# Graph attention and experts on one Trainium2 core: TensorE works in even steps of two second-layer tiles, two picked columns and one first-layer slice, with one signal per step

## The reference

```python
# x: 6250 x 256; 100000 edges src -> dst
x = x + gnn(layernorm(x))              # graph attention, 4 heads of 64
xn = layernorm(x)                      # what both parts below start from
# a second graph attention makes the expert scores, 4 heads x 4 experts
h = (xn @ W_gat).reshape(M, 4, 4)
e = leaky_relu(a_src[src] + a_dst[dst]); alpha = softmax of e over the edges with one dst
agg = segment_sum(h[src] * alpha, dst) + b_gat
scores = layernorm(agg, ln_gamma, ln_beta).reshape(M, 4, 4).mean(1)
w, i = softmax(top_2(scores))
for ei in range(4):                    # the experts, 256 -> 512 -> 256
    g = w where i == ei
    out += g * (gelu(xn @ W1[ei] + b1[ei]) @ W2[ei] + b2[ei])
return x + out
```

## Time and profile before

| what | value |
|---|---|
| median of 3 runs | 4049.74 us (4045.44 to 4051.8) |
| the profiled execution | 4058.66 us, its span 4057.0 us |
| busy in the span | PE 1940.2 us (48%), DVE 1968.4 (49%), POOL 1737.6 (43%), ACT 663.5 (16%) |
| stretch of the 7 rounds | 2071 us to 3776 us |
| last units after the rounds | 3776 us to 3896 us |

### The profile page before, as it was taken

The page is one execution under the profiler, slowest core; times in us unless marked ns, Lnnn a source line. Parts: engine busy times, 40 slices in busy tenths (PEclk is TensorE's granted clock), DMA queues, the critical chain, the costliest instruction groups (busy, mean ns, idle before and its releaser), DMA issues.

```text
span 4057.0 us, 25978 instructions
## 1 busy us (share of the span) xinstructions
PE 1940.2 (48%) x7318; PEld 1438.6 (35%) x7322; DVE 1968.4 (49%) x3777; ACT 663.5 (16%) x1401; POOL 1737.6 (43%) x1787
## 2 busy tenths in 40 slices
PE   4415044444334353546541395554657565556425
PEld 3311033233223132324430374443546454444314
DVE  7876776645656653446520163233334343233646
ACT  7300021122112121212310011010101011011003
POOL 0015765655565444540777314344442424343241
PEclk9758566666666676767565697777878787777757
DMA  3211344544455343434621011111110111111415
GB/s 123 36 48 28 87 157 152 164 155 154 137 170 164 113 145 121 160 116 168 178 77 8 13 37 27 26 22 22 31 31 29 28 31 25 24 22 25 180 55 211
DMA packets 154183, 354.73 MB, mean 87 GB/s; under 512 B 55510, under 2 KB 96518, under 8 KB 144406
## 3 DMA queue, kind: packets, MB, share of 16 engines
q1 hardware_dynamic: 68303, 196.54, 13.5%
q0 software_dynamic: 69936, 121.07, 12.7%
q10 hardware_dynamic: 15866, 36.29, 2.3%
HBM read 181.01 MB, written 172.19 MB: 87 GB/s over the span
## 4 chain that ended last, share of the span: by engine, by line
PE 18%; another core or an unknown queue 16%; issue 10%; DVE 7%; ACT 1%; DMA 1%; POOL 0%; ACTq 0%; SPq 0%; DVEq 0%; POOLq 0%
PE ffn_psY L1512 7%; PE ffn_psH L1498 6%; PE pick_rows L858 3%; DVE pick_prod L888 1%; DVE at_ring L897 1%; DVE at_ring L692 1%; PE mid_psH L1424 1%; PE mid_psT L1181 1%; DVE pick_hot L874 0%; POOL acc L979 0%; DVE xnT L1715 0%; DVE at_high L662 0%; PE pick_node L839 0%; DVE at_ring L684 0%
## 5 line engine op out<-in xcount | busy, mean ns | idle before, releaser
L618 POOL DMA_INDIRECT at_ring<-table,e_col x768 | 725.9, 945 | 1061.2 <-DMA at_sums<-at_ring 831.2
L2057 POOL DMA_INDIRECT at_ring<-table,at_idx x693 | 671.9, 970 | 585.1 <-DMA at_sums<-at_ring 378.4
L2149 PE MATMUL at_psS<-at_ring,at_hot 128*128 128x260 f32 x1584 | 495.1, 475 | 437.4 <-issue 268.9
L1498 PE MATMUL ffn_psH<-xnT,ffn_space 128*128 x896 | 405.3, 605 | 452.5 <-ACT ffn_space L1539 289.4
L888 DVE SCALAR_TENSOR_TENSOR pick_prod<-const_iota,pick_tile,pick_rows 128x400 f32<-128x400 f16 x256 | 158.5, 629 | 831.1 <-remote 547.5
L2149 PEld LDWEIGHTS at_psS<-at_ring,at_hot 128*128 128x128 f32 x1584 | 346.9, 236 | 575.3 <-issue 351.3
L1512 PE MATMUL ffn_psY<-ffn_space 128*128 128x256 f32 x1568 | 387.7, 405 | 286.4 <-DVE ffn_space L1570 271.9
L1498 PEld LDWEIGHTS ffn_psH<-xnT,ffn_space 128*128 128x128 f32 x896 | 271.9, 312 | 553.8 <-ACT ffn_space L1539 301.0
L1512 PEld LDWEIGHTS ffn_psY<-ffn_space 128*128 128x128 f32 x1568 | 314.9, 204 | 345.8 <-DVE ffn_space L1570 285.8
L2171 ACT ACTIVATE at_ring<-at_psS 128x520 f32<-128x520 f32 (+1 forms) x432 | 238.7, 567 | 768.0 <-PE at_psS L2149 354.6
L1539 ACT ACTIVATE ffn_space<-ffn_psH,ffn_b 128x448 f32<-128x448 f32 x224 | 141.5, 634 | 1056.4 <-DMA at_sums<-at_ring 790.7
(11 more groups left out here) (404 smaller groups left out, 2432.6 us busy)
## 6 DMA issues: line engine op xcount, KB each, us to landing
at_sums<-at_ring SPq DMA_DIRECT2D x72, 1452.0 KB
products<-ffn_space ACTq DMA_DIRECT2D x28, 512.0 KB
at_ring<-table,e_col POOLq DMA_INDIRECT x867
at_sums<-at_ring SPq DMA_DIRECT2D x16, 768.0 KB, 3.2
late_space<-products SPq DMA_DIRECT2D x24, 512.0 KB, 7.9
at_ring<-table,at_idx POOLq DMA_INDIRECT x693
products<-ffn_space ACTq DMA_DIRECT2D x28, 384.0 KB
late_space<-products SPq DMA_DIRECT2D x24, 384.0 KB, 9.8
```

Source lines behind the costliest of these rows:

```text
L618: g.indirect_dma_start(self.ring[z][:, k, 0:TW], None, self.table, bass.IndirectOffsetOnAxis(ap=self.runs.col[:, u * U + k:u * U + k + 1], ...
L1498: last = pe.matmul(self.psH[part][:, 0:half], self.w1[:, k, e * HID + f:(e + 1) * HID:FT], self.xnT[:, k, bass.ds(r * (BT * P) + part * ha ...
L2057: g.indirect_dma_start(self.ring[z][:, k, 0:self.TW], None, self.table, bass.IndirectOffsetOnAxis(ap=self.idx[:, z, k:k + 1], axis=0)).the ...
L2149: last = pe.matmul(self.psS[at % 2][:, k - lo, 0:TW], self.hot[:, b, k, :], rows[:, b * self.SUB + k, 0:TW], start=True, stop=True)
```

## The change

PE's work of a round becomes 16 equal steps (`STEPS`). In step s it makes one pair of second-layer tiles of five steps earlier (`product`, `PAIRS`: 2, 2, 2 and 1 tiles, both tiles of a pair in one bank), then two picked columns, then slice s of the first layer (`hidden`), and raises one semaphore, `s_step`, once. ACT waits for it and does both gelus of the step; DVE waits for it and does the step's two picks (`take`), one addition over the pair (`add`), and the rest of the pick (`put`). `s_h`, `s_y`, `s_out` are gone, and `s_node` is raised only once, at the start. PE still waits for `s_hid`, `s_kept`, `s_hot` and `s_prod`, which ACT and DVE raise. The steps run on over the rounds' border (the second layer of a round's last expert is made in the next round); round 0 stands outside of the loop.

`weigh` is cut in two parts, and `scores` and `weigh` stand after other steps: for unit 2r - 1 after steps 3, 5 and 6 of round r, for unit 2r after steps 10, 11 and 13. Before, unit 2r was weighed at the start of round r + 1. After the rounds, six more steps finish the products, and the last 20 picked columns go four to a signal, over `pick_rows` and the two `psH` banks. SP's early loads for the mixing start after 14 stored units, not 12.

```diff
     def weigh(self, v, u):
+        self.weigh_first(v, u)
+        self.weigh_second(v, u)
+
+    def weigh_first(self, v, u):
...
-        last.then_inc(self.s_node, 1)
+        return last
...
-        for k in range(2 * half, 2 * half + 2):
-            self.column(pe, k, i % 2, k, r * self.ROUND + (i * self.COLS + k + 1))
-
-    def column(self, pe, n, z, k, kept):
+        for k in range(2):
+            pe.wait_ge(self.s_kept, r * self.ROUND + (slot * 2 + k + 1))
+            last = self.column(pe, self.ps_rows[k], i % 2, half * 2 + k)
+        return last
...
-        last.then_inc(self.s_out, 1)
-
-    def late_tensor(self, pe, rounds):
...
+        for k in range(self.COLS):
+            n = chunk * self.COLS + k
+            if not first or k < self.BANKS:
+                pe.wait_ge(self.s_kept, self.BANKS + n - (self.BANKS if first else self.COLS) + 1)
+            last = self.column(pe, banks[k], chunk % 2, k)
+        return last
...
+    def take(self, v, slot, banks):
+
+        S, D = self.SPAN, self.D
+        tiles = self.c["iota16"][:, 0:S].unsqueeze(1).to_broadcast([P, D, S])
+        for k in range(2):
+            n = slot * 2 + k
+            v.scalar_tensor_tensor(out=self.prod[:, k, :, :], in0=tiles, scalar=self.tile[:, n:n + 1],
+                                   in1=banks[k][:, 0:S * D].rearrange("p (d s) -> p d s", d=D),
+                                   op0=ALU.is_equal, op1=ALU.mult).then_inc(self.s_kept, 1)
+
+    def put(self, v, att, slot):
...
-    BT = 7
+    BT, LAG = 7, 5
     HALVES = ((0, 4), (4, 7))
+    PAIRS = ((0, 2), (2, 4), (4, 6), (6, 7))
...
+    def hidden(self, pe, r, s):
+
+        FT, K, BT, HID, half = self.FT, self.K, self.BT, self.HID, self.BT * P // 2
+        e, f = divmod(s, FT)
+        for part in range(2):
+            pe.wait_ge(self.s_hid, r * (2 * self.STEPS) + (2 * s + part + 1))
+            for k in range(K):
+                last = pe.matmul(self.psH[part][:, 0:half], self.w1[:, k, e * HID + f:(e + 1) * HID:FT],
+                                 self.xnT[:, k, bass.ds(r * (BT * P) + part * half, half)],
+                                 start=(k == 0), stop=(k == K - 1))
+        return last
+
+    def product(self, pe, r, n):
+
+        FT, DIM = self.FT, self.DIM
+        e, j = divmod(n % self.STEPS, FT)
+        lo, hi = self.PAIRS[j]
+        pe.wait_ge(self.s_prod, r * self.STEPS + (n + 1))
+        for t in range(lo, hi):
+            for f in range(FT):
+                last = pe.matmul(self.psY[j % 2][:, (t - lo) * DIM:(t - lo + 1) * DIM],
+                                 self.hid[:, e % 2, f, t * P:(t + 1) * P], self.w2[:, e * FT + f, :],
+                                 start=(f == 0), stop=(f == FT - 1))
+        return last
+
+    def tensor(self, pe, picks):
+
+        pe.wait_ge(self.s_w, 16 * (self.K + 1))
+        for s in range(self.STEPS):
+            if s == self.LAG:
+                pe.wait_ge(self.s_w2, 16)
+            if s >= self.LAG:
+                self.product(pe, 0, s - self.LAG)
+            self.hidden(pe, 0, s)
+            picks(0, s).then_inc(self.s_step, 1)
+        with pe.Fori(1, self.rounds) as r:
+            for s in range(self.STEPS):
+                self.product(pe, r, s - self.LAG)
+                picks(r, s)
+                self.hidden(pe, r, s).then_inc(self.s_step, 1)
+
+    def end_tensor(self, pe, s):
+
+        if s == self.LAG - 4:
+            self.freed_by_scalar(pe)
+        self.product(pe, self.rounds, s - self.LAG)
...
+        for s in range(self.STEPS):
+            self.activate(a, 0, s)
+            beside(0, s)
+            if s > self.LAG:
+                self.store(a, 0, s - self.LAG - 1)
+        with a.Fori(1, self.rounds) as r:
+            for s in range(self.STEPS):
+                self.activate(a, r, s)
+                beside(r, s)
+                self.store(a, r, s - self.LAG - 1)
...
+    def activate(self, a, r, s):
+        half = self.BT * P // 2
+        e, f = divmod(s, self.FT)
+        a.wait_ge(self.s_step, r * self.STEPS + (s + 1))
+        for part in range(2):
+            a.activation(self.hid[:, e % 2, f, part * half:(part + 1) * half], self.psH[part][:, 0:half],
+                         ACT.Gelu, bias=self.b1[:, s:s + 1]).then_inc(self.s_hid, 1)
+
+    def store(self, a, r, n):
+
+        e, j = divmod(n % self.STEPS, self.FT)
+        if j % 2:
+            (lo, hi), s_kept = self.HALVES[j // 2], self.s_kept[j // 2]
+            a.wait_ge(self.s_prod, r * self.STEPS + (n + 3))
+            a.dma_start(self.products[bass.ds(r + n // self.STEPS, 1), :, e, lo:hi, :].rearrange("o p t d -> (o p) t d"),
+                        self.prod[:, lo:hi, :]).then_inc(s_kept, 16)
...
+    def add(self, v, n):
+
+        e, j = n // self.FT, n % self.FT
+        lo, hi = self.PAIRS[j]
+        if j % 2 == 0:
+            v.wait_ge(self.s_kept[j // 2], 16 * e + 16)
+        v.tensor_tensor(self.prod[:, lo:hi, :], self.psY[j % 2][:, 0:(hi - lo) * self.DIM].rearrange("p (t d) -> p t d", d=self.DIM),
+                        self.b2[:, e % self.E, :].unsqueeze(1).to_broadcast([P, hi - lo, self.DIM]), ALU.add)\
+            .then_inc(self.s_prod, 1)
...
-                        att.sync(sp, lambda: mix.begin(sp, ffn), ffn.rounds * 2 - 2)
+                        att.sync(sp, lambda: mix.begin(sp, ffn), ffn.rounds * 2)
...
+                        def step(i):
+                            v.wait_ge(ffn.s_step, i + 1)
+                            pick.take(v, i, pick.ps_rows)
+                            if 0 <= i - ffn.LAG < ffn.steps:
+                                ffn.add(v, i - ffn.LAG)
+                            pick.put(v, att, i)
+
+                        def late_chunk(c):
+                            v.wait_ge(ffn.s_step, slots + c - slots // 2 + 1)
                             for half in range(2):
-                                ffn.vector(v, r, e, half)
-                                picked()
+                                pick.take(v, 2 * c + half, late_banks[2 * half:2 * half + 2])
+                                pick.put(v, att, 2 * c + half)
 
                         for r in range(ffn.rounds):
-                            hidden((lambda: att.weigh(v, 2 * r - 2)) if r else None)
-                            hidden(None, (lambda: att.scores(v, 2 * r - 1)) if r else None)
-                            products(r, 0)
-                            hidden(None, (lambda: att.weigh(v, 2 * r - 1)) if r else None)
-                            products(r, 1)
-                            if r == 0:
-                                spread.vector(v)
-                            hidden(None, lambda: att.scores(v, 2 * r))
-                            products(r, 2)
-                            products(r, 3)
+                            for s in range(ffn.STEPS):
+                                step(r * ffn.STEPS + s)
+                                if r and s == 3:
+                                    att.scores(v, 2 * r - 1)
+                                if r and s == 5:
+                                    att.weigh_first(v, 2 * r - 1)
+                                if r and s == 6:
+                                    att.weigh_second(v, 2 * r - 1)
+                                if r == 0 and s == 9:
+                                    spread.vector(v)
+                                if s == 10:
+                                    att.scores(v, 2 * r)
+                                if s == 11:
+                                    att.weigh_first(v, 2 * r)
+                                if s == 13:
+                                    att.weigh_second(v, 2 * r)
...
+                        for i in range(ffn.steps, slots):
+                            step(i)
+                            if i == ffn.steps:
+                                att.scores(v, last - 2)
+                            if i == ffn.steps + 2:
+                                att.weigh_first(v, last - 2)
+                            if i == ffn.steps + 3:
+                                att.weigh_second(v, last - 2)
+                        chunks = range(slots // 2, pick.chunks)
+                        for c in chunks:
+                            late_chunk(c)
+                            if c == chunks[1]:
+                                att.scores(v, last - 1)
+                            if c == chunks[2]:
+                                att.weigh(v, last - 1)
```

More of the change, by code:

```diff
@@ L812, in table_vector @@
         v.wait_ge(self.s_att, 16)
+        v.wait_ge(self.s_node, 1)
         self.hots(v, 0)
@@ L2725, in gnn_moe_kernel @@
                           [ring[:, :, :].rearrange("p u w -> p (u w)") for ring in att.ring])
+                late_banks, slots = pick.ps_rows + ffn.psH, ffn.steps + ffn.LAG + 1
+                assert slots % 2 == 0 and slots < 2 * pick.chunks
                 with nc.Block() as block:
@@ L2865, in _ @@
                     def _(pe):
```

(2 more changed lines are left out.)

157 lines of the change are left out of this document (41 added, 116 removed).

## The result

The changed kernel takes 3931.48 us (median of 4 runs, 3923.27 to 3956.72), the one before 4048.77 in the same measurement: a ratio of 0.972 (95% interval 0.968 to 0.977). The forecast was 3720, with a range of 3560 to 3870. The direction and the length of the fast steps held; the gain is 117 us where 329 were forecast.

The account below looks back on a forecast made before the run. It took PE's signals, arriving 11.2 us each during POOL's gather bursts, as the bound. Gains of 115 (start), 202 (five rounds) and 20 (end), total 337, gave 3722, 3713 on the runs' scale, stated as 3720; range 3560 to 3870.

Parts of the forecast that it names:

- The fast step: A step of the rounds outside slow gather stretches: PE's work without waits, 124 us a round, 7.8 us a step.
- (c): Rival, between bursts: lockstep stretches each step to 9.5 us through DVE's fullest steps or short waits; 3840 us, chance 0.09.
- (d): Rival, all steps: PE idling a little in each step stays at 1.2 GHz, 15.6 us of matmuls a step; 4240 us, chance 0.03.
- The slow step: A step during a gather burst: signal 11.2 us, DVE's read 0.63, picks and slice 4.7, slow clock about 2; together 18.5 us.
- 3.0 steps are slow: Steps passing in the 56 us slow part of each burst, each 10.7 us longer than a fast one; a round about 190 us.
- start: Stretch up to the burst following unit 1's weighing, before at 2520.79 us, forecast at 2406: gain 115 us.
- five rounds: The rounds from 2520.79 to 3673.29 us: 1152.5 us become 5 x 190 = 950, gain 202 us.
- end: From 3673.29 us to the last unit's scores: 222.5 us become 203, gain 20 us.
- (b): Rival, steps in bursts: a step costs two places of the grid, 30 us, a round 208; 3860 us, chance 0.12.
- (a): Rival, steps in bursts: 11.2 us is only spacing, so a slow step takes 11.2 us; 3480 us, chance 0.13.
- (e): Rival, bursts: signals do not cause slow stretches, the change saves only their handling, within 15 us; 4035 to 4050 us, chance 0.03.
- Wrong altogether: Sign against the whole forecast: in bursts, the 11.2 us would depend on the matmuls or the reader, not on the signal.

Follow-up runs that it names:

- more_signals: The changed kernel with 4.5 more signals in each step of rounds 1 and up, awaited by nobody, same matmuls: 3938.47 us, 0.9745 of the kernel before.
- the spaced kernel: The changed kernel with two waited memsets between two gathers, units from the fourth on: 3615.85 us (0.9022 of the kernel before) on a holding chip, 3083.89 (1.1205) on a free one.

## Why the prediction was wrong

**The bound, read rightly.** That TensorE, ScalarE and VectorE wait for one another in GpSimd's bursts, and that the bursts are the cause, held: with the gathers gone a round falls from 215.6 to 122.6 us.

**The fast step, right.** 7.8 us was forecast; the gapless rounds give 122.6 / 16 = 7.7, with the lockstep hidden and the clock at 1.00. Rivals (c) and (d) fell.

**The slow step, wrong, and with it the size.** The step that failed reads "So during gathers PE's signals arrive one at a time, 11.2 us each". Each of the kernel before's signals stood behind four records, and 4 x 2.80 = 11.2; rows that hold only such signals can't tell the two apart. Two of my own rows spoke against it: the 20.6 us of the earlier trace rows with no visible signal in them, close to the 22.4 of a tile of `psY` with its 8 records, and the 14.0 us of a lone signal, five times 2.80. I took both for scatter. From there the sum follows wrongly: a slow step of 18.5 us (measured 29.7 and 31.7 in a short burst, 44.8 to 88 in the long one), "3.0 steps are slow" (measured two signals), a round of 190 (215.6). In the sum: start 115 forecast, 50 measured; five rounds 202, measured 74; end 20, measured 11. That the time fell at all was forecast for a reason that did not hold: with 72 signals a round put back the gain stays (0.9745). The direction was luck.

**The rivals.** (b), 30 us a slow step and 3860 us, has the length of a step in a short burst, for the wrong reason; its time is still 71 us low, 26 of it at the start and 38 in the five rounds. (a), one signal every 11.2 us, fell with the price itself. (e), that count buys nothing, has the right mechanism, by more_signals, and the wrong time: it overlooked that fewer waits let more records into a slow stretch. The sentence "Wrong altogether would be a cause of the 11.2 us that depends on the matmuls" named what came.

**The rule that I weighed.** The 26.3 ns for a signal in the Trainium skill, TensorE: Matmul & The Clock Gate, section The cost: per-tile semaphore tail, were nearer to the 11 ns that the extra signals measured (0.8 us for 72) than the price I put in their place.

**Open.** Why some chips hold records and others don't, and whether the same chip always does; whether TensorE is held when no profile is taken; what in GpSimd's close gathers does it; at which spacing it begins; which part of the change brings the 11 us on a free chip, or lets more records into a slow stretch on a holding one; and why the stretch ahead of the rounds ends up to 40 us earlier or later from one profile to the next.

## What to carry to other kernels

A regular delay in a trace is a price per something: list what lies between two places of the grid (signals, matmuls, columns, bytes) and look for the rows in which these differ, before summing; here the irregular rows held the answer. A tiny added operation, one kind at a time, tells the candidates apart in one run each. And measure on more than one chip: nine tenths of this change's gain stand only on the holding ones, and the spaced kernel gains 10% there and loses 12% on the others.

## What the runs showed of the hardware

On three of seven chips, as they were when met and in profiled executions, TensorE completes one matmul record every 2.80 us, of 16 or of 448 columns alike, from some 9 us into a row of GpSimd's gathers 1.25 us apart; it runs on about 30 records ahead and then stands. The hold ends 3 us after a burst of 60 us and 18 us after one of 200. Most landings of the gathers are missing from the profile meanwhile (126 to 139 of 768 recorded). On the other four the kernels ran without it; the trace with all gathers, on one of them, shows TensorE busy all through beside them. Gathers 1.81 us apart hold nothing on a holding chip either (tried on one), nor do SyncE's transfers of the same size (on another).
